# First attention of a two-layer decoder: queries in four column groups over all keys, sums turned by transposes, sixteen exponential buffers, maxima split on GpSimd

## What is computed

```python
x = x + _L0_attn_ref(_layernorm(x), ...)
# inside, B = 2 batches, H = 16 heads, d = 16 channels a head, no mask:
q, k, v = heads(x @ Wq), heads(x @ Wk), heads(x @ Wv)
attn = softmax((q1 @ k_eff1.T + q2 @ k_eff2.T) * h ** -0.5)    # 1024 x 1024 for each of the 32 heads
out = (attn @ v) merged over heads @ Wo
```

## Time and profile before

| | us |
|---|---|
| three runs, median (lowest, highest) | 1811.63 (1809.51, 1814.55) |
| the profiled execution, time | 1812.42 |
| its span, first to last instruction | 1810.6 |
| heads of the first attention, exponential phase | 87.9 to 506.3 |
| a head in the steady state | 12.97 |
| first rows stored by SP after the attention (L461); first use of the retention weights (L1527) | 567.8; 1184.1 |
| granted TensorE clock, mean over the span | 0.939 |

### The profile page before, as it was taken

How to read it: one execution, slowest core, us unless ns; L and a number is a source line. 1 busy time by engine, 2 the same in 40 slices (tenths; PEclk the granted TensorE clock), 3 DMA queues, 4 the chain that set the end, 5 groups by cost and what they waited for, 6 DMA issues and landing times. The chain is left out here.

```text
span 1810.6 us, 29293 instructions
## 1 busy us (share of the span) xinstructions
PE 1581.6 (87%) x9415; PEld 1054.8 (58%) x9416; DVE 1023.1 (57%) x2024; ACT 601.4 (33%) x1167; POOL 407.9 (23%) x839
## 2 busy tenths in 40 slices
PE   6899999999979941899999999879987838999996
PEld 5433333333346731677777777646656627999995
DVE  7678888888549967211112111278878854444442
ACT  3267777777735520111111111033345510000000
POOL 1000000000014410342222211146652212333331
PEclk9799999999989975899999999989999958999997
DMA  2112221111400120133222331110024115666673
GB/s 72 38 38 64 52 55 40 42 40 43 154 27 25 36 65 1 44 99 90 50 67 90 98 84 15 20 42 1 2 68 142 36 59 171 183 189 175 177 182 101
DMA packets 89222, 134.90 MB, mean 75 GB/s; under 512 B 17712, under 2 KB 66224, under 8 KB 88976
## 3 DMA queue, kind: packets, MB, share of 16 engines
q1 hardware_dynamic: 73968, 113.08, 19.9%
q0 software_dynamic: 15168, 20.72, 7.2%
HBM read 98.04 MB, written 20.84 MB: 66 GB/s over the span
## 5 line engine op out<-in xcount | busy, mean ns | idle before, releaser
L2094 DVE TENSOR_REDUCE mx<-ps 128x1 f32<-128x1024 f32 x256 | 306.1, 1217 | 57.9 <-PE ps L2203 57.9
L1993 ACT ACTIVATE turns_of_use<-ps 128x512 f32<-128x512 f32 x512 | 281.5, 596 | 130.5 <-PE ps L2210 128.4
L1285 PE MATMUL ps<-xTe,wide 128*128 128x320 f32 x1024 | 279.4, 435 | 1.0 <-issue 1.0
L1285 PEld LDWEIGHTS ps<-xTe,wide 128*128 128x128 f32 x1024 | 195.5, 191 | 82.0 <-issue 2.6
L1352 DVE TENSOR_TENSOR hTe<-prT,ps 128x320 f32<-128x320 f32 x128 | 62.4, 487 | 214.4 <-ACT prT L1324 209.1
L2210 PE MATMUL ps<-QS,KS 99*128 99x512 bf16 x512 | 163.1, 387 | 6.8 <-ACT turns_of_use L1993 4.7
L507 POOL TENSOR_TENSOR nv<-nv 128x2 f32<-128x2 f32 (+2 forms) x84 | 18.1, 216 | 643.7 <-DVE nv L692 639.2
L2203 PE MATMUL ps<-KS,QS 96*128 96x512 bf16 x512 | 144.2, 395 | 9.7 <-DVE mx L2094 6.9
L1293 PE MATMUL ps<-wide,hTe 128*128 128x256 f32 x640 | 141.4, 380 | 8.7 <-DVE hTe L1352 8.7
L1442 PEld LDWEIGHTS ps<-xw_all,w1t 128*128 128x128 f32 x1248 | 145.3, 192 | 3.7 <-issue 1.0
L1459 PE MATMUL ps<-wide,hTm 128*128 x624 | 144.1, 385 | 3.4 <-DVE hTm L1489 3.4
(11 more groups left out here) (313 smaller groups left out, 2174.7 us busy)
## 6 DMA issues: line engine op xcount, KB each, us to landing
w1t<-in_L_ffn_w SPq DMA_DIRECT2D x39, 1024.0 KB
wide<-in_L_ffn_gate_weight SPq DMA_DIRECT2D x8, 1024.0 KB
wide<-_L_ffn_ff_pre_act_weight SPq DMA_DIRECT2D x8, 1024.0 KB
wide<-L_ffn_ff_post_act_weight SPq DMA_DIRECT2D x8, 1024.0 KB
wide<-in_L_ffn_w SPq DMA_DIRECT2D x1, 8192.0 KB, 27.3
QS<-wide SPq DMA_DIRECT2D x192, 32.0 KB, 2.0
KS<-wide SPq DMA_DIRECT2D x192, 32.0 KB, 2.0
VS<-V_all SPq DMA_DIRECT2D x32, 128.0 KB, 2.1
```

What stands on the lines that cost most here:

```text
L1285: ins = pe.matmul(ps[:, 3 + 2 * (q % 2) + n, 0:HC], wt[:, k, f * P:f * P + P], xTe[:, k, hf * HC:hf * HC + HC], start=(k == 0), stop=(k == ...
L1993: act.activation(PT[:, q % 8, :], ps[:, 4 + q % 2, :], ACT.Exp).then_inc(h_e.sem, 1)
L2094: v.tensor_reduce(mx[:, s, t:t + 1], ps[:, 2 * (t % 2):2 * (t % 2) + 2, :], AX.XY, ALU.max).then_inc(h_rm.sem, 1)
```

## The change

In the first attention only:

- `weigh` handles a range of key tiles. The four column groups are now four quarters of the queries (256 columns each), each over all keys: four matmuls of 256 columns a key tile. A head has three calls: tiles 0 to 2, 3 to 5, and 6 and 7 (these in the next head).
- There are 16 exponential buffers instead of 8, the new ones in the last 4096 columns of `wide`. ACT waits for the weighing of the head before instead of that of eight exponentials ago.
- The four groups need no adding: `evac` copies 256 columns instead of 512, and `turn_sums` is two fp32 transposes instead of four matmuls against `sel`. `sel` and its DMA are gone.
- `split_max` moves from DVE to POOL, in five steps of two-operand arithmetic.
- The order on PE within a head is changed.
- `sp_retention` comes behind the meeting of all engines instead of ahead of it.

```diff
-        PT = turns_of_use[:].rearrange("p (q s) -> p q s", q=8)
+        PT = [m.rearrange("p (q s) -> p q s", q=8) for m in (turns_of_use[:], wide[:, 12288:16384])]
-        h_pv = sig("h_pv", 16)
+        h_pv = sig("h_pv", 8)
...
+            meet(sp, 1)
             sp_retention(sp)
-            meet(sp, 1)
...
+            def split_max(n, s):
+                pool.wait_ge(h_rm.sem, h_rm.upto(n))
+                pool.wait_ge(h_mt.sem, h_mt.upto(n - 2))
+                none = zeros[:, 0:1].to_broadcast([P, TB])
+                c(pool.tensor_tensor(mpart[:, s, 0, :], none, mx[:, s, :], ALU.subtract))
+                c(pool.tensor_tensor(mleft[:, 0, :], mx[:, s, :], mpart[:, s, 0, :], ALU.add))
+                c(pool.tensor_tensor(mpart[:, s, 1, :], none, mleft[:, 0, :], ALU.subtract))
+                c(pool.tensor_tensor(mleft[:, 1, :], mleft[:, 0, :], mpart[:, s, 1, :], ALU.add))
+                pool.tensor_tensor(mpart[:, s, 2, :], none, mleft[:, 1, :], ALU.subtract).then_inc(h_mp.sem, 1)
...
-                    act.wait_ge(h_pv.sem, h_pv.upto(n, q - 7))
-                    act.activation(PT[:, q % 8, :], ps[:, 4 + q % 2, :], ACT.Exp).then_inc(h_e.sem, 1)
+                    act.wait_ge(h_pv.sem, h_pv.upto(n - 1, q // 2 + 1))
+                    act.activation(PT[q // 8][:, q % 8, :], ps[:, 4 + q % 2, :], ACT.Exp).then_inc(h_e.sem, 1)
...
-                act.copy(Osb[:], ps[:, 6, :]).then_inc(h_ev.sem, 1)
+                act.copy(Osb[:], ps[:, 6, 0:256]).then_inc(h_ev.sem, 1)
...
-            def weigh(n, sl, t):
-                pe.wait_ge(h_e.sem, h_e.upto(n, 2 * t + 4))
-                for q in range(4):
-                    pe.matmul(ps[32 * q:32 * q + 32, 6, :], VS[:, sl, t + q // 2, :], PT[:, (2 * t + q) % 8, :],
-                              start=(t == 0), stop=(t == TB - 2)).then_inc(h_pv.sem, 1)
+            def weigh(n, sl, t0, t1):
+                pe.wait_ge(h_e.sem, h_e.upto(n, 2 * t1))
+                for t in range(t0, t1):
+                    for g in range(4):
+                        q = 2 * t + g // 2
+                        ins = pe.matmul(ps[32 * g:32 * g + 32, 6, 0:256], VS[:, sl, t, :],
+                                        PT[q // 8][:, q % 8, (g % 2) * 256:(g % 2) * 256 + 256],
+                                        start=(t == 0), stop=(t == TB - 1))
+                    ins.then_inc(h_pv.sem, 1)
...
-                for j in range(4):
-                    ins = pe.matmul(ps[:, 7, j * 64:j * 64 + 64], Osb[:, j * P:j * P + P], sel[:],
-                                    start=True, stop=True)
+                for j in range(2):
+                    ins = pe.transpose(ps[:, 7, j * P:j * P + P], Osb[:, j * P:j * P + P], ident[:])
```

More of the change, by code:

```diff
@@ L205, in decoder @@
         VS = sbA("VS", [P, 4, TB, 32])
-        Osb = sbA("Osb", [P, 512])
+        Osb = sbA("Osb", [P, 256])
         mx = sbA("mx", [P, 2, TB])
-        mneg = sbA("mneg", [P, 2, TB])
+        mleft = sbA("mleft", [P, 2, TB])
         mpart = sbA("mpart", [P, 2, 3, TB], BF16)
         mrow = sbA("mrow", [24, 2, P], BF16)
-        sel = sbA("sel", [P, 64])
-        rec = sbA("rec", [P, 4, 2])
+        rec = sbA("rec", [P, 2, 4])
         TWO_ONES = float(np.array(0x3F803F80, np.uint32).view(np.float32))
@@ L428, in decoder @@
         A_LOADS = 6 * 16
-        W_LOADS = 6 * 16
+        W_LOADS = 5 * 16
         NLOAD = [0]
@@ L1862, in _ @@
                              (wkA, chunked(w["L0_attn_Wk"])), (wqA, chunked(w["L0_attn_Wq"])),
-                             (wvA, chunked(w["L0_attn_Wv"])), (sel[:], w["c_sel"])):
+                             (wvA, chunked(w["L0_attn_Wv"]))):
                 sp.dma_start(dst, src).then_inc(w_part, 16)
@@ L1948, in _ @@
             pool.wait_ge(v_set, 1)
+            def split_max(n, s):
[7 more added lines that the diff above has]
+                pool.tensor_tensor(mpart[:, s, 2, :], none, mleft[:, 1, :], ALU.subtract).then_inc(h_mp.sem, 1)
+            with c.fori(B * H // 2, 2 * 4) as i:
+                for s in range(2):
+                    split_max(2 * i + s, s)
             meet(pool, 1)
@@ L2115, in normalise @@
                 v.wait_ge(h_fin.sem, h_fin.upto(n))
-                y = ps[:, 7, 0:256].rearrange("p (j c d) -> p j c d", j=4, c=2)
+                y = ps[:, 7, 0:256].rearrange("p (j c d) -> p j c d", j=2, c=4)
                 c(v.reciprocal(rec[:].unsqueeze(3), y[:, :, :, DH:DH + 1]))
                 o = O_all[:, bass.ds((n // H) * TB, TB), bass.ds((n % H) * DH, DH)]\
-                    .rearrange("p (c j) d -> p j c d", c=2)
-                v.tensor_tensor(o, y[:, :, :, 0:DH], rec[:].unsqueeze(3).to_broadcast([P, 4, 2, DH]),
+                    .rearrange("p (c j) d -> p j c d", c=4)
+                v.tensor_tensor(o, y[:, :, :, 0:DH], rec[:].unsqueeze(3).to_broadcast([P, 2, 4, DH]),
                                 ALU.mult).then_inc(h_no.sem, 1)
@@ L2125, in head @@
                     maxima(n + 2, hh % 2, 0, 1)
-                if not (last and hh == 3):
-                    split_max(n + 1, (hh + 1) % 2)
                 if not (last and hh >= 2):
@@ L2139, in _ @@
             maxima(0, 0, 0, 8)
-            split_max(0, 0)
             maxima(1, 1, 0, 6)
@@ L2145, in _ @@
                 head(n, n, 0, n == 0)
-            with c.fori(B * H // 4 - 2, 4 * 5) as i:
+            with c.fori(B * H // 4 - 2, 4) as i:
                 for hh in range(4):
@@ L2212, in scores_t, with turn_sums @@
                   .then_inc(h_st.sem, 1)
[L2214 to L2221 removed]
+            def weigh(n, sl, t0, t1):
[7 more added lines that the diff above has]
+                    ins.then_inc(h_pv.sem, 1)
+            def turn_sums(n):
                 pe.wait_ge(h_ev.sem, h_ev.upto(n))
                 pe.wait_ge(h_no.sem, h_no.upto(n - 1))
[L2225 to L2228 removed]
+                for j in range(2):
+                    ins = pe.transpose(ps[:, 7, j * P:j * P + P], Osb[:, j * P:j * P + P], ident[:])
                 ins.then_inc(h_fin.sem, 1)
@@ L2253, in head @@
                 if not first:
-                    weigh(n - 1, (sl + 3) % 4, 6)
+                    weigh(n - 1, (sl + 3) % 4, 6, 8)
                 scores_t(n, sl, 1, 0)
@@ L2259, in head @@
                 if not first:
-                    sum_tiles(n - 1)
+                    pe.wait_ge(h_mc.sem, h_mc.upto(n))
+                    turn_sums(n - 1)
                 scores_t(n, sl, 2, 1)
                 scores_t(n, sl, 3, 0)
+                ahead_scores(2)
+                scores_t(n, sl, 3, 1)
+                scores_t(n, sl, 4, 0)
                 pe.wait_ge(h_ev.sem, h_ev.upto(n - 1))
[L2264 to L2267, removed]
+                weigh(n, sl, 0, 3)
                 scores_t(n, sl, 4, 1)
-                weigh(n, sl, 2)
                 scores_t(n, sl, 5, 0)
-                scores_t(n, sl, 5, 1)
                 if not (last and hh == 3):
@@ L2274, in head @@
                 ahead_scores(4)
+                scores_t(n, sl, 5, 1)
                 scores_t(n, sl, 6, 0)
                 scores_t(n, sl, 6, 1)
-                weigh(n, sl, 4)
+                weigh(n, sl, 3, 6)
                 scores_t(n, sl, 7, 0)
+                ahead_scores(6)
                 scores_t(n, sl, 7, 1)
-                ahead_scores(6)
             pe.wait_ge(ones_set, 1)
@@ L2295, in _ @@
                 head(B * H - 4 + hh, hh, B * H // 4 - 1, False, True)
[L2296 to L2302, removed]
+            weigh(B * H - 1, 3, 6, 8)
+            turn_sums(B * H - 1)
             meet(pe, 1)
```

9 lines of the change are left out of this document (removed).

## The result

| | before | after |
|---|---|---|
| median of four runs each (lowest, highest), us | 1811.46 (1809.51, 1814.55) | 1833.22 (1830.27, 1836.53) |
| ratio to before, with its 95% interval | | 1.0122 (1.0106 to 1.0139) |
| span of the profiled execution, us | 1810.6 | 1832.3 |
| a head in the steady state, us | 12.97 | 13.77 |

A forecast was written before the change was run, and what follows sets the result against it. TensorE (PE) was taken as the bound. A head's work of 11.85 us plus waits of 1.83 made 13.68, taken as +0.69 on 12.97; 29 heads gave +20.0, the last two -0.6: 1831 us, range 1820 to 1840.

The forecast's parts named there:

- The two waits of 0.64 behind ACT: PE ahead of exponential scores 13 and 1, third in a row: waits 1.08 - 0.44 = 0.64 us each, per head.
- The wait of 0.38 ahead of tile 3: PE reaches tile 3's maximum scores at x + 2.67, DVE's reduces allow x + 3.05: 0.38 us a head.
- Weighing: PE's weighing in a head: calls of 1.42, 1.42 and 1.00 us instead of 4.40 in all, saving 0.24.
- The sums: PE's turning of the sums by fp32 transposes: some 0.50 us instead of 0.93, saving 0.43 a head.
- The wait ahead of number 6: PE ahead of exponential score 6, behind score 4's exponential: round of 1.16 us against 0.98, wait 0.17 a head.
- The buffers: The 16 exponential buffers free nothing by themselves; they let a weighing call wait until three tiles are there.
- POOL: Five split steps of 0.25, 1.3 us, ready some 5 us early: cost 0, bound +0.3 us a head.
- SP's round: Fetch to landed row of maxima, 10.5 us after the weighing: hidden with 0.9 to spare, binding under 12.1 to 12.8.
- The clock: Full clock forecast; rival: PE's clock falls to half in the heads, 1867 to 1871 us, 4%.
- PE does not stand still: Rival: exponentials and maxima return before PE asks, 1786 to 1792 us; with its partial case (1795), 9%.
- DVE is not late: Rival: the 0.38 us wait for DVE's reduces vanishes, +0.31 a head, 1820 us; 8%.
- all exponentials answer at 0.50: Rival: exponentials 11 and 15 also start 0.50 after their matmul, +0.16 a head, 1836 us (1840 with POOL's bound); 10%.

The follow-up runs named there:

- e1: The changed kernel with exponential score 15 moved ahead of the last maximum scores (tiles 6 and 7); 1812.71 us, ratio 1.0009 to before.
- e4: The changed kernel with the splitting of the maxima back on DVE, between the reduces of tiles 0 and 1; 1888.61 us, ratio 1.0417 to before.
- e3: The changed kernel with PE's old order and four two-tile weighing calls, the first moved ahead of exponential score 6; 1789.45 us, ratio 0.9866 to before.
- e5: e3 with the splitting of the maxima back on DVE; 1791.73 us, ratio 0.9878 to before.
- e7: e3 with 8 exponential buffers instead of 16; 1789.47 us, ratio 0.9875 to before.
- e9: e4 with exponential score 15 moved ahead of the last maximum scores; 1858.81 us, ratio 1.0257 to before.

## Why the prediction was right, point by point

The mechanism was right: three of the four waits, in place and size. Two terms were mis-sized and cancelled each other, and several small ones that the text left out did so in part; that the total came within 2 us is partly luck.

- **What bounds the kernel.** Right. PE's start-to-start times in the attention's heads carry the whole difference.
- **The two waits of 0.64 behind ACT.** Right, 0.63 each. e1 took one of them away and nothing else, and 0.59 a head went.
- **The wait of 0.38 ahead of tile 3.** Right, 0.37; and with the split on DVE 1.38 for the 1.4 given. What that wait would do to the clock was not in the text: the prediction put the worth of moving the split to POOL at that one wait, and it was twice as much (e4).
- **Weighing.** Calls of 1.44 (314.02 to 315.46, and one from 318.41), 1.44 and 1.00 (322.33 to 323.33), for 1.42, 1.42 and 1.00: right to 0.04 in a head.
- **The sums: mis-sized.** The prediction read four records of fp32 transposes as two transposes, put 0.43 on them, and added 0.07 for a change of operands: 0.50. They are four transposes, one record each, 0.11 apart. Two take 0.22 (311.09 to 311.31), and no change of operands shows. The term was 0.28 too high. Rows 7 could have told: its "x8" of L894 are the eight transposes that the loops of `turn_probs` issue, one record each. The sentence "an fp32 matmul leaves two records" is true of the weighing and not of a transpose.
- **The wait ahead of number 6: mis-sized by the same error, the other way.** The round of that bank was worked out as 1.16 and is 1.15. Since the sums fill 0.28 less of it, the wait is 0.49 instead of 0.17, 0.32 more. A saving in front of a wait for another engine moves into that wait. The two errors cancel in the total, so the total does not prove the two terms; the rows at 311.09 to 312.02 do, and e3, in which the 0.49 is gone.
- **The head.** 11.65 of work for 11.85 (0.28 from the sums, less 0.08 spread over the rest) and 2.12 of waits for 1.83: 13.77 for 13.68. The allowance of 0.03 for the method's own error went the wrong way. Against the 13.66 taken that is 0.11 a head, 3.1 us. A further 1.0 us: the prediction counted only the last two heads as short, while before, the two ahead of them were short too (12.61 each, without the wait ahead of tile 5) and are full now, and the first few were short by 0.3 together.
- **Against it** stood 1.2 us in front of the first copy and 0.7 in the rest. Neither was in the text, and no cause is shown: over the twelve traces the first copy comes anywhere from 99.7 to 105.0 us, at 100.8 in e5, where the split is on DVE. The sum of these, +21.7 for +19.4, is the 2 us between forecast and measurement.
- **The buffers.** Right for an order with calls of two tiles (e7).
- **POOL.** The five steps, in the timeline of POOL:

```profile
309.46 0.20 POOL L1954 TENSOR_TENSOR mpart<-zeros,mx 128x8 bf16<-128x8 f32 x1 [12.45 <-DVE mx L2108]
...
310.57 0.20 POOL L1958 TENSOR_TENSOR mpart<-zeros,mleft 128x8 bf16<-128x8 f32 x1
```

  They start 0.28 apart for the 0.25 given, end at 310.77, and PE turns the maxima at 315.99: 5.2 us ahead, as forecast. They slow no reduce. In e3 they lie right across the first of two, in the timeline of DVE and POOL:

```profile
286.88 0.20 POOL L1954 TENSOR_TENSOR mpart<-zeros,mx 128x8 bf16<-128x8 f32 x1 [10.93 <-DVE mx L2108]
...
287.25 2.36 DVE L2108 TENSOR_REDUCE mx<-ps 128x1 f32<-128x1024 f32 x2 [0.53 <-PE ps L2203]
...
287.99 0.20 POOL L1958 TENSOR_TENSOR mpart<-zeros,mleft 128x8 bf16<-128x8 f32 x1
...
293.54 2.36 DVE L2108 TENSOR_REDUCE mx<-ps 128x1 f32<-128x1024 f32 x2
```

  Two reduces take 2.36 with POOL at work beside the first and 2.36 without. The Trainium skill (SBUF — State Buffer, "Who interferes with whom") states that a tensor_reduce never contends with GpSimd on trn2; by that rule the cost is 0, and the trace agrees. The bound of +0.3 a head was not needed.
- **SP's round.** Hidden, as forecast. It starts at 309.69 and the row of maxima is issued at 317.86, from SP's queue in after:

```profile
309.69 0.53 SPq L1881 DMA_DIRECT2D QS<-wide  x1
...
317.86 0.78 SPq L1888 DMA_DIRECT2D QS<-mrow  x1
```

  With the 2.1 to landing it is there at 320.0. The next head's first score is the second of the two from 320.94, at 321.16: a margin of 1.2 for the 0.9 worked out. The estimate that it would bind in a head under 12.1 to 12.8 fits e3: with heads of 12.2 it binds four times among the first and then no more.
- **The clock.** Right that it holds in after. The rival's mechanism was real: e4 shows it one move away from this kernel, and e9 two.
- **The rivals.** "PE does not stand still" (1786 to 1792) fell for this order; it is close to what e3 reached (1789) once the order lets PE run. "DVE is not late" and "all exponentials answer at 0.50" fell with the 0.37 and the two 0.63.

## What to carry to other kernels

An order in which the bound engine issues k pieces to an engine that has k - 1 banks costs the round trip less the issue time at each such place: count the issue time between two uses of one bank (here 1.08 to 1.15 us are needed, 0.44 stood there), and put other work of the bound engine in between before making any of its pieces cheaper. When a piece is made cheaper, look at the next wait behind it: 0.49 of the 0.71 saved on the sums came back as a wait until a weighing was moved into the gap. Undo the parts one by one: here a good one (the sums, -0.7 us of work a head) and a bad one (the order, +1.1) were in one change.

## What the runs showed of the hardware that was not expected

- **The clock falls within a loop of short waits.** In e4 PE waits about 3 us of a 14.7 us head (in pieces of 1.4 and less), and the granted clock goes to 0.5 for 3.4 us at a time, 17 times in 29 heads, each costing 1.6 us. In e9, about 2.4 of 14.1 us, 7 times. In after, 2.1 of 13.8 us, and in e1, 1.5 of 13.2: never in those heads. The Trainium skill (TensorE: Matmul & The Clock Gate, "A second HAM failure mode: psum-queue depth-cycling") describes such oscillation where PE idles shortly between groups as it goes round PSUM banks; e4 and e9 agree with that, after and e1 show that such waits need not bring it. These are three kernels of one kind, and no bound is worked out from them.
- **An fp32 transpose of 128x128 leaves one record and holds PE 0.11 us** (311.09 to 311.31 for two), while an fp32 matmul of the weighing leaves two records.
- **A DVE reduce of 1024 columns from PSUM takes 1.2 us whether POOL is at work or not**, although two small DVE instructions beside POOL's fills took 4.32, one of them 4.00, while the other fifteen of line L480 take 0.40 to 0.42 each.
